# A hand-written step planner gets another transfer model, other durations, another order of bank choices and new weights, in an eight-layer hybrid transformer kernel

## The chip, the cores and the metric

One core of one Trainium2 chip runs the whole program. The metric is the device time of one execution in microseconds (us); lower is better. The names of the engines are those of the profile: PE is TensorE (PEld its weight loads), DVE is VectorE, ACT is ScalarE, POOL is GpSimd, SP is SyncE, whose only work here is to issue DMAs.

## The reference, cut to what matters

The input x has 4 batches of 1024 tokens with 128 features. Eight layers follow one another, each a residual around a layer norm, an attention or a feed-forward:

```
x = x + attn_a(layernorm(x))          # "full": 16 heads of 8, every query sees every key
x = x + ffn(layernorm(x))             # "ffn1": 128 -> 512 -> 128, relu
x = x + attn_b(layernorm(x))          # "causal" then "local" (window 32), 16 query and 4 key heads, rope, q and k normed
x = x + ffn(layernorm(x))             # "ffn2"
x = x + attn_padded(layernorm(x))     # "padded": window 32, 16 query and 2 key heads
x = x + moe(layernorm(x))             # "moe1": 8 experts, the best 2 for each token, width 352
x = x + attn_sink(layernorm(x))       # "sink": window 128 and 4 sink keys, 8 query and 4 key heads of 16
x = x + moe(layernorm(x))             # "moe2"
```

The batches do not depend on one another; the layers of one batch do.

## The kernel before, in words

`streams` describes the work of each batch as steps. A step (`Step`) has a list of pieces `on`, each an engine with a duration in nanoseconds, signals that it needs, and buffers that it takes from rings (`Ring`). `Plan.run` is a list scheduler that runs in Python while the program is built. It walks through its own time, and whenever an engine is free it picks, among the pieces that are ready and whose buffers can be had, the one that `urgency` puts highest. The order in which it picks becomes the order of the instructions in the queue of each engine, and the buffers that it picks are the ones that are used. On the chip the engines then run these queues in order and wait for semaphores. The plan's times are not used on the chip, only its orders, its choices of buffers and one more thing: where the plan sees PE idle, `tensor_program` puts matmuls on zeros (`nothing`, L1005 and L1007), one for each planned 230 ns after the first 200 or 450, at most 8 in a gap after the first 90 us.

`urgency` compares in this order: `short` (the engine of the step's next piece is about to run dry, by `SHORT`), then `step.far + step.lead + WORTH * stays`. `far` is the longest chain of planned durations and landings from the step to the end, in ns, so at most a few million. `lead` is 1000 times the sum of a number for the layer and batch (`LEADS`) and one for the kind of step (`URGENT`), so tens of millions. `WORTH` is a bonus for a PE step in the array mode that PE is in.

Transfers are planned in `Plan.go`. A step with DMAs gives for each the number of DMAs, a latency `ns` and an occupation `moved`. `moving` is the time at which the transfers planned so far are through:

```
for name, n, ns, moved in step.dmas(step):
    step.signals["dma"].name = name
    self.moving = max(self.moving, at) + moved
    self.due(step.signals["dma"], 16 * n, self.moving + ns)
```

Here `now` is when the issuing piece starts and `at` when it ends.

PSUM has 8 banks. `RB` gives pairs of neighbouring banks (for `scores` and `top`), and of the free pairs it takes the one free for longest. `RP` gives single banks from 7 downwards, for the accumulator `po` into which all products of a half unit of attention go. `RA` gives single banks from 7 downwards for short uses. All three share the same banks. `Step.room` goes through the rings of a step in the order in which they are named, so a ring that is named first chooses first.

An attention layer of a batch has 4 units. A unit is loaded (`load`, queries and keys from DRAM, where `split_out` put them as three bf16 parts), then in full, padded and sink the row maxima are found (`top` on PE at L1154 with its mask at L1134 or L1141, and `top` on DVE at L1609), then `scores` (PE L1185, mask L1134 or L1141) is followed by the exponential (ACT L1367), and `product` (PE L1205) adds up in `po`.

An experts layer (moe1, moe2) sorts the tokens of a batch into 23 tiles of 128 slots: 16 `scatter` DMAs by POOL (L1840), each pair after the one before has landed; `slot_load` brings 4 tiles from DRAM into a PT buffer (L1928), `slot_turn` transposes them (PE L1242, ACT L1384 into one of 3 SG buffers), `weights` brings each tile its expert (L1943, 384 KB), `up` (PE L1254, ACT L1389, DVE L1734 and L1737) and `down` (PE L1271, ACT L1402 into the same SG buffer) compute, `back` by POOL (L1848) scatters the rows to DRAM. An SG buffer is free when its `back` DMAs have landed. At the end `rows_in` (L1949) and `combine` (DVE L1745) add the rows to x. `zero` clears the slots in DRAM once for each batch (L1921).

Of the kernel before, what the change touches and what calls it, by code (L numbers as in the profile page):

```python
# [19 lines left out]
LEADS = dict(full=(33216, 19541, 25084, -10647), ffn1=(48012, -1595, 43514, 121701), causal=(-4228, -29528, -5475, 14633), local=(-22242, 1197, 39634, -30739), ffn2=(27232, 109504, 17203, 84270), padded=(6306, -51060, -19639, -27531), moe1=(7879, -27871, -29235, -11132), sink=(60610, 10946, -47942, -4076), moe2=(-46608, -58920, -16653, -27602))  # L20
URGENT = dict(back=13314, biased=-16184, combine=-8366, consts=50459, dest=-41354, divide_causal=-43734, divide_full=-14494, divide_local=-17929, divide_padded=-6368, divide_sink=-16411, down=32076, experts_in=-57783, gate_exp=-42278, gate_w=20450, k_padded=-30673, kv_global=-18223, latent=42087, load_causal=53214, load_full=-79031, load_local=-25554, load_padded=17122, load_sink=55523, mbd=6258, mixed=1379, narrow=2211, norm=-22134, ones=-2965, out=-4598, padding=41178, product_causal=158, product_full=33757, product_local=-27607, product_padded=-18694, product_sink=41317, project_causal=-26349, project_full=-64094, project_local=-22717, project_padded=188, project_sink=-10415, q_global=-64125, qk_rstd=-56931, qk_scaled=15461, qk_squares=-14285, qkv=-9555, ranks=-35465, residual=38685, route=-17061, rows_in=-41517, rstd=6282, scaled=-7356, scaled_dirs=-45906, scatter=-48392, scores_causal=13672, scores_full=807, scores_local=-10944, scores_padded=-11578, scores_sink=-265, sink_v=-6569, slot_load=53327, slot_turn=-10741, split_all=53562, split_hi=26458, split_lo=12833, split_out_causal=50567, split_out_full=-30502, split_out_local=-43483, split_out_padded=27921, split_out_sink=7305, squares=-60664, stats=-11217, store=-43970, top_full=8113, top_padded=-73, top_sink=7265, tops_full=-51182, tops_out_full=-35060, tops_out_padded=31757, tops_out_sink=-98863, tops_padded=352, tops_sink=-7328, tops_turn=82199, turn=11184, turn_add=6718, turn_mul=1696, up=-16818, v_full=10032, v_padded=54237, weights=17671, widen=24704, with_h=45447, zero=-17655)
SHORT = dict(pe=23620427, act=1123, dve=1280, pool=7696641590, sp=2084661)
ISSUE = 500
SWITCH = 100
WORTH = 2171223
# [89 lines left out]
class Plan:  # L115
# [3 lines left out]
    def __init__(self):  # L119
        self.count, self.order, self.steps = {}, {e: [] for e in ENGINES}, []  # L120
        self.free, self.ready, self.times = {e: 0 for e in ENGINES}, {e: [] for e in ENGINES}, set()
        self.banks = {}
        self.look, self.lead, self.coming, self.mode, self.moving = {}, 0, {e: 0 for e in ENGINES}, "whole", 0
# [16 lines left out]
    def add(self, *args, **given):  # L140
        step = Step(*args, **given)
        attention = step.given.get("A")
        step.lead = self.lead + 1000 * URGENT.get(step.kind + "_" + attention.name if attention else step.kind, 0)
# [14 lines left out]
    def urgency(self, step, i, now):  # L158
# [5 lines left out]
        return short, step.far + step.lead + WORTH * stays, -step.index  # L164

    def go(self, step, i, now):
# [1945 lines left out]
```

## Time and profile before

| | |
|---|---|
| median of 3 runs | 2376.72 us (2367.81 to 2389.58) |
| the profiled execution: its time, its span | 2365.46 us, 2363.7 us |
| PE busy | 2149.6 us (91%) |
| DVE busy | 1641.8 us (69%) |
| ACT busy | 1422.7 us (60%) |
| POOL busy | 674.2 us (29%) |
| share of the DMA engines' time, SP's queue | 31.5% |

The profile comes from one execution, whose span is from its first to its last instruction. An engine counts as busy while an instruction runs on it; the matmuls on zeros count as busy PE too. The idle time of an engine is put down to the instruction that came after it and to what released that instruction.

### The profile page before, as it was taken

What the parts mean: (1) busy time and instruction counts of PE and PEld (TensorE: products, weight loads), DVE (VectorE), ACT (ScalarE), POOL (GpSimd) and SP (SyncE); (2) the same over time, 40 slices, a digit from 0 to 9 for tenths busy, and PEclk for the clock granted to TensorE, in tenths of its full rate; (3) what the DMA queues carried; (4) which work ended last, traced back from release to release, by engine and by line L of the source; (5) the groups of instructions that cost most, each with busy time, mean ns of one, the idle gap of its engine ahead of it and who ended that gap; (6) DMA issues with size and microseconds to landing.
All of it is one profiled execution on the core that took longest, in us unless ns stands there. A gap on an engine that the chain in (4) does not pass through costs nothing.

```text
span 2363.7 us, 62948 instructions
## 1 busy us (share of the span) xinstructions
PE 2149.6 (91%) x26220; PEld 1224.9 (52%) x26243; DVE 1641.8 (69%) x3685; ACT 1422.7 (60%) x2105; POOL 674.2 (29%) x602
## 2 busy tenths in 40 slices
PE   7788988898999999899999999999999999999987
PEld 3222232223224233334554566697766887777987
DVE  9998879998876683423453388468687776866755
ACT  1367766666786889998777745644455234444333
POOL 4400000012002001203224214355515555424553
PEclk9999999999999999999999999999999999999998
DMA  6701100101121112112313324465624675634776
GB/s 189 222 18 35 41 17 17 44 17 50 27 50 45 25 34 65 51 23 68 92 47 87 78 48 113 106 204 158 184 50 117 188 222 168 192 101 123 229 240 195
DMA packets 160746, 235.23 MB, mean 100 GB/s; under 512 B 21968, under 2 KB 81872, under 8 KB 160208
## 3 DMA queue, kind: packets, MB, share of 16 engines
q1 hardware_dynamic: 145456, 206.81, 31.5%
q0 software_dynamic: 9984, 20.73, 2.5%
q8 instruction: 209, 3.42, 0.6%
q10 hardware_dynamic: 5024, 3.67, 0.6%
q14 instruction: 73, 0.60, 0.1%
HBM read 156.28 MB, written 73.88 MB: 97 GB/s over the span
## 4 chain that ended last, share of the span: by engine, by line
PE 56%; DVE 14%; ACT 11%; issue 7%; POOL 6%; DMA 5%; SPq 1%; POOLq 0%; DVEq 0%; ACTq 0%
PE PS L1205 16%; ACT PT L1367 10%; PE PS L1185 8%; DVE MS L1609 7%; PE PS L1154 5%; PE PS L1254 5%; DMA scr_y<-XN,SL 3%; PE PS L1141 3%; PE PS L1271 3%; PE PS L1054 2%; PE PS L1044 2%; POOL scr_o L1848 2%; PE PS L1015 2%; POOL scr_y L1840 2%; PE PS L1215 2%
## 5 line engine op out<-in xcount | busy, mean ns | idle before, releaser
L1367 ACT ACTIVATE PT<-PS 128x1024 f32<-128x1024 f32 (+5 forms) x1200 | 1018.6, 911 | 392.8 <-PE PS L1185 378.8
L1609 DVE TENSOR_REDUCE MS<-PS 128x2 f32<-128x1024 f32 (+3 forms) x736 | 778.2, 1097 | 141.4 <-PE PS L1154 136.1
L1205 PE MATMUL PS<-PT,VA 128*9 128x512 f32 (+7 forms) x6720 | 558.8, 434 | 14.3 <-ACT PT L1367 12.0
L1185 PE MATMUL PS<-QO,KO 64*64 64x512 bf16 (+7 forms) x6240 | 420.0, 305 | 47.0 <-ACT PT L1367 29.6
L1185 PEld LDWEIGHTS PS<-QO,KO 64*64 64x64 bf16 (+2 forms) x6240 | 177.5, 105 | 271.6 <-ACT PT L1367 130.9
L1154 PE MATMUL PS<-KO,QO 61*64 61x512 bf16 (+2 forms) x3520 | 286.4, 326 | 34.0 <-DVE MS L1609 16.6
L1254 PE MATMUL PS<-SG,WB 128*128 128x128 f32 x2208 | 276.1, 278 | 6.2 <-DMA WB<-in_mW 2.9
L1254 PEld LDWEIGHTS PS<-SG,WB 128*128 128x128 f32 x2208 | 261.8, 194 | 12.1 <-issue 7.3
L1154 PEld LDWEIGHTS PS<-KO,QO 61*64 61x64 bf16 (+1 forms) x3520 | 126.1, 104 | 243.4 <-DVE MS L1609 127.3
L1848 POOL DMA_INDIRECT scr_o<-SG,TO x184 | 182.0, 989 | 226.6 <-ACT SG L1402 197.4
L1205 PEld LDWEIGHTS PS<-PT,VA 128*9 128x9 f32 (+2 forms) x6720 | 127.8, 90 | 177.0 <-issue 115.4
L1788 POOL MEMSET VA<- 128x32 f32 (+2 forms) x20 | 3.7, 187 | 715.2 <-PE PS L1205 715.2
L1141 PE MATMUL PS<-c_half 64*64 64x128 bf16 (+4 forms) x2560 | 165.4, 279 | 24.0 <-ACT PT L1367 13.2
L1271 PE MATMUL PS<-W,HM 128*128 x1104 | 158.7, 283 | 16.8 <-DVE HM L1737 13.1
L1734 DVE SCALAR_TENSOR_TENSOR HM<-HM,PS 128x384 f32<-128x384 f32 x184 | 100.9, 548 | 94.8 <-ACT HM L1389 94.6
L1641 DVE RECIPROCAL RC<-PS 128x16 f32<-128x16 f32 x144 | 36.2, 252 | 178.9 <-PE PS L1215 178.8
L1840 POOL DMA_INDIRECT scr_y<-XN,SL x128 | 124.2, 971 | 122.3 <-DMA scr_y<-XN,SL 60.5
L1389 ACT ACTIVATE HM<-PS 128x384 f32<-128x384 f32 x184 | 90.4, 491 | 112.8 <-PE PS L1254 112.3
L1271 PEld LDWEIGHTS PS<-W,HM 128*128 128x128 f32 x1104 | 139.0, 194 | 26.3 <-issue 25.3
L1402 ACT ACTIVATE SG<-PS 128x128 f32<-128x128 f32 x184 | 51.1, 277 | 167.9 <-PE PS L1271 167.2
L1141 PEld LDWEIGHTS PS<-c_half 64*64 64x64 bf16 x2560 | 64.9, 104 | 145.9 <-ACT PT L1367 74.9
L1373 ACT ACTIVATE OB<-PS 128x512 f32<-128x512 f32 x144 | 88.0, 611 | 65.9 <-PE PS L1205 65.5
(182 smaller groups left out, 2474.7 us busy)
## 6 DMA issues: line engine op xcount, KB each, us to landing
WB<-in_mW SPq DMA_DIRECT2D x184, 384.0 KB
PT<-scr_y SPq DMA_DIRECT2D x40, 264.0 KB, 4.6
PT<-scr_o SPq DMA_DIRECT2D x16, 512.0 KB, 5.3
QO<-scr_q_full SPq DMA_DIRECT2D x32, 192.0 KB
KO<-scr_k_full SPq DMA_DIRECT2D x32, 192.0 KB
QO<-scr_q_causal SPq DMA_DIRECT2D x32, 192.0 KB
QO<-scr_q_local SPq DMA_DIRECT2D x32, 192.0 KB
QO<-scr_q_padded SPq DMA_DIRECT2D x32, 192.0 KB
```

The source lines that it names most:

```text
L1141: mm(pb[64 * c:64 * c + 64, h2, at:at + copies * width], C["identw"][r, :], rows, start=i == 0, stop=False, skip_group_check=True)
L1154: p = mm(pb[c:c + n, h2, at:at + kn], q[:, 128 * tt + c:128 * tt + c + n], k[:, k0:k0 + kn], start=not masked, stop=True, skip_group_check ...
L1185: p = mm(pb[c:c + n, h2, at:at + tn], k[:, k0 + c:k0 + c + n], q[:, t0:t0 + tn], start=not masked, stop=True, skip_group_check=masked)
L1205: p = mm(bank[32 * h:32 * h + D + 1, c0:c0 + tn], va[0:n, :], pt[0:n, plane, at:at + tn], start=s["first"] and j == 0, stop=s["last"] and ...
L1254: p = mm(pb[:, k, 128 * c:128 * c + 128], wt[:, at:at + 128], y, start=True, stop=True)
L1271: p = mm(RA[s.use["bank"].i][:, 0:128], hm[:, 128 * c:128 * c + 128], W3[:, bass.ds(first + 128 * c, 128)], start=c == 0, stop=c == 2)
L1367: e = activation(pt[0:r, 0:n, a:b], ps[0:r, 0:n, a:b], ACT.Exp, scale=s["A"].scale)
L1389: activation(HM[s.use["hm"].i][:, :], pair(s)[:, 0, 0:DW], ACT.Tanh, scale=0.5).then_inc(S["up_tanh"], 1)
L1609: v.tensor_reduce(to, got, AX.X, ALU.max).then_inc(S["top"], 1)
L1734: last(v.scalar_tensor_tensor(hm, hm, 1.0, pb[:, 0, 0:DW], ALU.add, ALU.mult))
L1840: p.indirect_dma_start(scr_y[b], bass.IndirectOffsetOnAxis(ap=SL[b][:, c, i:i + 1], axis=0), XN[:, i, 0:ROW], None).then_inc(S[s.signals[" ...
L1848: p.indirect_dma_start(scr_o[b], bass.IndirectOffsetOnAxis(ap=TO[b][:, t:t + 1], axis=0), SG[s["yt"].i][:, at:at + 128], None).then_inc(S[ ...
```

## The change

Transfers: the occupation now starts when the issuing piece starts (`now`), and the latency is added to the later of the end of the issue and the end of the occupation. The numbers of nearly all transfers change. Durations: `up` on PE from 1340 to 1385 ns, `down` from 670 to 755, and `product` 30 ns more for each block of keys after the first. Banks: the first `scores` of a chain names its accumulator ahead of its pair. Weights: all of `LEADS`, `URGENT`, `SHORT` and `WORTH` are new. `CHANGED` is empty and adds nothing; `lead` is computed from `plan.layer` and comes to the same formula. No instruction is added to or taken from a step; orders, buffers and matmuls on zeros follow from the plan.

```diff
-LEADS = dict(full=(33216, 19541, 25084, -10647), ffn1=(48012, -1595, 43514, 121701), causal=(-4228, -29528, -5475, 14633), local=(-22242, 1197, 39634, -30739), ffn2=(27232, 109504, 17203, 84270), padded=(6306, -51060, -19639, -27531), moe1=(7879, -27871, -29235, -11132), sink=(60610, 10946, -47942, -4076), moe2=(-46608, -58920, -16653, -27602))
+LEADS = dict(full=(53341, 36548, 37095, 4161), ffn1=(2644, -19651, 48946, 155384), causal=(5626, -23700, -8138, 18246), local=(-32503, 3959, -15293, -35192), ffn2=(34227, 133518, 50757, 136545), padded=(20383, -47193, 15851, 10637), moe1=(-10457, -25159, -18591, -12001), sink=(104327, 44402, -48211, 33771), moe2=(-57924, -103913, 2283, -11110))
+STRETCH, CHANGED = 100000, {}
...
-SHORT = dict(pe=23620427, act=1123, dve=1280, pool=7696641590, sp=2084661)
+SHORT = dict(pe=267476623, act=1084, dve=1269, pool=9525014120, sp=120267)
...
-WORTH = 2171223
+WORTH = 6579224
...
-                self.moving = max(self.moving, at) + moved
-                self.due(step.signals["dma"], 16 * n, self.moving + ns)
+                self.moving = max(self.moving, now) + moved
+                self.due(step.signals["dma"], 16 * n, max(self.moving, at) + ns)
...
-                    dmas=lambda s: [("%s_out%s" % (what, b), 3, 1500, 12 * r * n // 450)])
+                    dmas=lambda s: [("%s_out%s" % (what, b), 3, 1700, 3500 * r * n // 131072)])
...
-                        s = add("scores", cost, dict(load=U["load"]), dict(bank=RB, pt=PT, **chain) if po is None else dict(bank=RB, pt=PT),
+                        s = add("scores", cost, dict(load=U["load"]), dict(**chain, bank=RB, pt=PT) if po is None else dict(bank=RB, pt=PT),
...
-                    p = add("product", [("pe", int(1.667 * w) + 17, "product")], dict(v=v_ready, exp=[x["exp"] for x in was]), order=last,
+                    p = add("product", [("pe", int(1.667 * w) + 17 + 30 * (len(g["blocks"]) - 1), "product")], dict(v=v_ready, exp=[x["exp"] for x in was]), order=last,
...
-                        dmas=lambda s, n=n: [("q_in%s" % s.use["qo"].i, n, 1600, 4000 if not A.tiled else 2900 if A.group == 1 else 1800)])
+                        dmas=lambda s, n=n: [("q_in%s" % s.use["qo"].i, n, 1800, 7800 if not A.tiled else 6000 if A.group == 1 else 4500)])
```

The other new numbers, latency and occupation in ns, before and after; the issue is the duration of the issuing piece:

| step | issue | latency, occupation before | after |
|---|---|---|---|
| `zero` | 6000, then 500 | 15000, 0 | 1800, 5600 |
| `consts` | 1000 | 3000, 11000 | 1800, 7000 |
| `experts_in` | 500 | 3000, 9000 | 1900, 4600 |
| `scatter` | 2210 | 1500, 100 | 1500, 300 |
| `slot_load` | 500 | 2900, 900 | 1900, 1200 |
| `weights` | 450 | 1900, 1400 | 2100, 1300 |
| `back` | 960 | 2000, 50 | 1500, 300 |
| `rows_in` | 500 | 3000, 1850 | 2100, 2200 |
| `store` | 500 | 3000, 2000 | 2100, 1500 |

In `URGENT` 80 numbers change; of those that the text speaks of, `top_full` goes from 8113 to 18606, `split_hi` from 26458 to 55531, `scores_causal` from 13672 to 20993.

## Rows read from the trace of the kernel before

**Rows 1.** The page, busy time of each engine over the span

```profile
PE 2149.6 (91%) x26220; PEld 1224.9 (52%) x26243; DVE 1641.8 (69%) x3685; ACT 1422.7 (60%) x2105; POOL 674.2 (29%) x602
```

**Rows 2.** Busy time by stretch: stretch, length, then the engines

```profile
0.00:40.00 40.00, 25.93 (x139) 15.67 (x139) 35.38 (x124) 8.23 (x13) 15.88 (x21) 1.00 0.59 148
40.00:100.00 60.00, 46.51 (x326) 13.99 (x326) 59.12 (x64) 11.89 (x14) 34.74 (x16) 0.97 0.90 277
100.00:500.00 400.00, 348.06 (x3409) 100.54 (x3409) 352.23 (x427) 268.63 (x284) 9.34 (x10) 1.00 0.14 32
...
1700.00:2200.00 500.00, 474.32 (x5736) 383.31 (x5748) 374.89 (x1170) 217.24 (x402) 212.72 (x211) 0.99 0.50 148
...
2300.00:2364.00 64.00, 48.45 (x429) 47.53 (x427) 34.73 (x86) 19.97 (x50) 23.08 (x25) 0.89 0.65 199
```

**Rows 3.** The same stretches, matmuls on zeros alone (PE, PEld, POOL)

```profile
0.00:40.00 40.00, 10.55 (x43) 4.38 (x43) 0.21 (x1) 1.00 0.59 148
40.00:100.00 60.00, 21.04 (x67) 5.89 (x67) 0.00 (x0) 0.97 0.90 277
100.00:500.00 400.00, 23.80 (x74) 5.14 (x73) 0.00 (x0) 1.00 0.14 32
...
sum 2364.00, PE 81.31 PEld 23.90 POOL 0.21; mean PE 8.13 PEld 2.39 POOL 0.02
```

**Rows 4.** Waits of PE over the span: us in total, times, longest

```profile
PE PS L1185 <- ACT PT L1367: 29.6, 74, 1.5
...
PE PS L1154 <- DVE MS L1609: 16.6, 52, 0.7
PE PS L1154 <- ACT PT L1367: 13.6, 21, 0.9
PE PS L1141 <- ACT PT L1367: 13.2, 39, 0.6
PE PS L1271 <- DVE HM L1737: 13.1, 10, 3.9
PE PS L1185 <- DVE MS L1609: 12.2, 31, 0.6
...
PE PS L1134 <- ACT SG L1384: 4.9, 2, 3.8
...
PE PS L1242 <- DMA PT<-scr_y: 3.4, 1, 3.4
...
PE PS L1254 <- DMA WB<-in_mW: 2.9, 3, 1.4
PE PS L1254 <- ACT SG L1384: 2.6, 2, 2.4
```

**Rows 5.** Waits of ACT over the span

```profile
ACT SG L1384 <- DMA scr_o<-SG,TO: 30.7, 14, 5.0
```

**Rows 6.** The page, DMA issues: count, size, median us from issue to landing

```profile
PT<-scr_y SPq DMA_DIRECT2D x40, 264.0 KB, 4.6
PT<-scr_o SPq DMA_DIRECT2D x16, 512.0 KB, 5.3
...
scr_y<-HM SPq DMA_DIRECT2D x4, 1518.0 KB, 8.1
```

**Rows 7.** Line L1928, the 48 slot loads

```profile
DMA to landing us min/median/max: 2.6/4.6/7.2
```

**Rows 8.** Chain that ended last, 2291 to 2301 us: start, us, what

```profile
2291.07 4.74 DMA WB<-in_mW
...
2298.56 1.34 PE PS L1254 x12
2299.90 0.67 PE PS L1271 x6
```

**Rows 9.** Timeline of PE, 2282 to 2289 us: start, us, instruction, idle before

```profile
2282.43 1.64 PE L1271 MATMUL PS<-W,HM 128*128 x6 [3.89 <-DVE HM L1737]
...
2283.86 2.38 PE L1254 MATMUL PS<-SG,WB 128*128 128x128 f32 x12
...
2286.75 1.50 PE L1254 MATMUL PS<-SG,WB 128*128 128x128 f32 x12
```

More of the change, by code:

```diff
@@ L22 @@
-SHORT = dict(pe=23620427, act=1123, dve=1280, pool=7696641590, sp=2084661)
+LEADS = dict(full=(53341, 36548, 37095, 4161), ffn1=(2644, -19651, 48946, 155384), causal=(5626, -23700, -8138, 18246), local=(-32503, 3959, -15293, -35192), ffn2=(34227, 133518, 50757, 136545), padded=(20383, -47193, 15851, 10637), moe1=(-10457, -25159, -18591, -12001), sink=(104327, 44402, -48211, 33771), moe2=(-57924, -103913, 2283, -11110))
+STRETCH, CHANGED = 100000, {}
+URGENT = dict(back=6321, biased=12423, combine=-30114, consts=71223, dest=-35934, divide_causal=-46876, divide_full=-14842, divide_local=-10228, divide_padded=5133, divide_sink=-25331, down=54974, experts_in=-45597, gate_exp=-19345, gate_w=43937, k_padded=-27108, kv_global=-36694, latent=37451, load_causal=55136, load_full=-98931, load_local=-64659, load_padded=44073, load_sink=48910, mbd=-27211, mixed=-22633, narrow=-21902, norm=-11253, ones=-381, out=-2013, padding=50769, product_causal=784, product_full=28059, product_local=-33836, product_padded=-9477, product_sink=32951, project_causal=-43056, project_full=-57538, project_local=-19091, project_padded=11700, project_sink=-12956, q_global=-85021, qk_rstd=-44870, qk_scaled=14611, qk_squares=-18579, qkv=-47915, ranks=-56805, residual=23888, route=-33480, rows_in=-59941, rstd=23560, scaled=1588, scaled_dirs=-66840, scatter=-25435, scores_causal=20993, scores_full=3298, scores_local=-8686, scores_padded=-15878, scores_sink=-8616, sink_v=7800, slot_load=67324, slot_turn=-4593, split_all=44198, split_hi=55531, split_lo=7723, split_out_causal=78242, split_out_full=-8892, split_out_local=-44055, split_out_padded=47993, split_out_sink=15080, squares=-68676, stats=-14713, store=-17676, top_full=18606, top_padded=7164, top_sink=1941, tops_full=-42818, tops_out_full=-29746, tops_out_padded=25651, tops_out_sink=-100701, tops_padded=-14612, tops_sink=-13606, tops_turn=86466, turn=19652, turn_add=18956, turn_mul=-11213, up=-26800, v_full=3177, v_padded=54005, weights=34310, widen=31222, with_h=32524, zero=11167)
@@ L122, in __init__ @@
         self.banks = {}
-        self.look, self.lead, self.coming, self.mode, self.moving = {}, 0, {e: 0 for e in ENGINES}, "whole", 0
+        self.look, self.layer, self.coming, self.mode, self.moving = {}, None, {e: 0 for e in ENGINES}, "whole", 0
     def given(self, name, value, at):
@@ L142, in add @@
         attention = step.given.get("A")
-        step.lead = self.lead + 1000 * URGENT.get(step.kind + "_" + attention.name if attention else step.kind, 0)
+        step.name, step.layer = step.kind + "_" + attention.name if attention else step.kind, self.layer
+        step.lead = 1000 * (LEADS[step.layer[0]][step.layer[1]] if step.layer else 0) + 1000 * URGENT.get(step.name, 0)
         self.steps.append(step)
@@ L163, in urgency @@
         stays = engine == "pe" and step.mode[0] == self.mode
-        return short, step.far + step.lead + WORTH * stays, -step.index
+        changed = CHANGED.get(now // STRETCH, {})
+        return short, step.far + step.lead + 1000 * (changed.get(step.name, 0) + changed.get(step.layer, 0)) + WORTH * stays, -step.index
     def go(self, step, i, now):
@@ L804, in experts @@
                 if t % GROUP == 0:
-                    load = add("slot_load", [("sp", ISSUE, "")], dict(y=placed), dict(pt=PT), leaves=dict(PT=2), b=b, t=t, n=n, dmas=lambda s, t=t: [("y_in%s_%s" % (b, t // GROUP), 1, 2900, 900)])
+                    load = add("slot_load", [("sp", ISSUE, "")], dict(y=placed), dict(pt=PT), leaves=dict(PT=2), b=b, t=t, n=n, dmas=lambda s, t=t: [("y_in%s_%s" % (b, t // GROUP), 1, 1900, 1200)])
                     s = add("slot_turn", [("pe", 110 * n, "slot_turn_mm"), ("act", 568 if n == GROUP else 465, "slot_turn")], dict(y=[load["dma"]]),
@@ L820, in experts @@
                 group["order"].append(s)
-                down = add("down", [("pe", 670, "down_mm"), ("act", 160, "rows")],
+                down = add("down", [("pe", 755, "down_mm"), ("act", 160, "rows")],
                            dict(src=[s["gated"]], w=experts_in, slots=slots),
@@ L826, in experts @@
                 s.use["hm"].give(down["down_mm"])
-                back = add("back", [("pool", 960, "")], dict(rows=[down["rows"]], to=[to["dest"]]), b=b, t=t, yt=group["yt"], dmas=lambda s: [("back%s" % s["yt"].i, 1, 2000, 50)])
+                back = add("back", [("pool", 960, "")], dict(rows=[down["rows"]], to=[to["dest"]]), b=b, t=t, yt=group["yt"], dmas=lambda s: [("back%s" % s["yt"].i, 1, 1500, 300)])
                 group["back"].append(back["dma"])
@@ L834, in experts @@
             for c in range(2):
[L835 removed]
+                got = add("rows_in", [("sp", ISSUE, "")], dict(rows=returned), dict(pt=PT), b=b, c=c, dmas=lambda s, c=c: [("g_in%s_%s" % (b, c), 1, 2100, 2200)])
                 s = add("combine", [("dve", 2200, "combine")], dict(got=[got["dma"]], w=wt, x=prev), b=b, c=c, pt=got.use["pt"])
@@ L841, in batch @@
         to_x = into_x()
-        plan.lead = 1000 * LEADS["full"][b]
+        plan.layer = ("full", b)
         attention(ATT["full"], lambda A: full_prologue(A, to_x), to_x)
         state["x"] = to_x["ready"]
-        plan.lead = 1000 * LEADS["ffn1"][b]
+        plan.layer = ("ffn1", b)
         feed_forward()
-        plan.lead = 1000 * LEADS["causal"][b]
+        plan.layer = ("causal", b)
         attention(ATT["causal"], causal_prologue, None)
-        plan.lead = 1000 * LEADS["local"][b]
+        plan.layer = ("local", b)
         attention(ATT["local"], local_prologue, None)
```

28 lines of the change are left out of this document (13 added, 15 removed).

## The prediction, made before any run of the changed kernel

> **What bounds the kernel now.** I read the busy shares first. PE is busy for 2149.6 us of 2363.7 [rows 1], so 214.1 us are idle. Of the busy time 81.3 us are matmuls on zeros, which the plan puts where it sees PE idle [rows 3]. PE's own work is thus 2149.6 - 81.3 = 2068.3 us, and 295.4 us of the span is PE time without work. The change leaves the work alone, so all that it can win or lose is in these 295.4 us. The reader should next see where they lie, from the table by stretch [rows 2] with the zeros beside it [rows 3]:
>
> - 0 to 100 us: idle 14.1 + 13.5, zeros 10.6 + 21.0, together 59.2. DVE is busy for 59.1 of the 60 us after 40, so the start is a chain of norms, splits and maxima on DVE.
> - 100 to 500 us: idle 51.9, zeros 23.8, together 75.7. DVE is busy for 352 of 400 us: the maxima of full attention.
> - 1700 to 2200 us: idle 25.7 in 500 us, 5%. The experts and the sink attention of different batches hide one another.
> - 2300 us to the end: 15.6 idle, nearly all of it after the last `down`, when only `back`, `rows_in`, `combine` and `store` are left.
>
> The rest, 295.4 - 59.2 - 75.7 - 25.7 - 15.6 = 119 us, is spread over the other stretches and the remaining zeros. Then I read what ended PE's waits [rows 4]. The costliest are waits for a bank pair or for an exponential: scores and maxima behind ACT L1367 or DVE L1609, 29.6 + 16.6 + 13.6 + 13.2 + 12.2 = 85.2 us. Waits that a landing ended itself are 3.4 + 2.9 = 6.3 us. Landings also act through ACT: `slot_turn` waits 30.7 us for the `back` DMAs that free its SG buffer [rows 5], the next tile's tanh stands behind it in ACT's queue, and PE's `down` behind that: 13.1 + 4.9 + 2.6 = 20.6 us [rows 4]. So what a wrong landing costs PE today is at most 6.3 + 20.6 = 27 us.
>
> **The change part by part.** The sum is made against the profiled execution, 2365.5 us, which is 11.3 us under the median of 2376.7; I add that back at the end.
>
> **Landings.** Both models can be worked out for a transfer that finds the queue empty, from the start of the issue. A load of full attention (6 issues of 500): before 3000 + 2900 + 1600 = 7500 ns, after max(6000, 3000) + 1800 = 7800. A `slot_load`: 500 + 900 + 2900 = 4300, after 1200 + 1900 = 3100. A `rows_in`: 5350, after 4300. A `weights`: 3750, after 3400. `zero`: 6000 + 15000 = 21000, after 7400. Against the trace: the `zero` landed in 8.1 us, so the new number is right where the old was far off; the slot loads landed in 4.6 us and `rows_in` in 5.3 at the median [rows 6], so there the old numbers are nearer and the new ones short by 1.5 and 1.0 us, unless the shared queue adds the rest. It can: the old occupation of a full load was 2.9 us, the new one is 6.0, so more transfers will find the queue taken. The fastest slot load took 2.6 us [rows 7], which says that an empty queue is quicker than either number.
>
> The Trainium skill (page "DMA: Bandwidth & Descriptors", section "Anatomy of one DMA — SWDGE (gpsimd) path") gives a fixed part of about 2.0 us and bytes over 436 GB/s, which by that rule makes an estimated 2.6 us for 264 KB. The trace agrees for the fastest slot load, 2.6 us [rows 7], and not for the median of 4.6 [rows 6]. If the rule were the whole truth, the new landings would be late enough everywhere and the rival below that loses by them would cost nothing.
>
> What the landings win: half of the 27 us above, 13, because orders that know when an SG buffer comes free put other work there, and because a wait can't vanish where POOL's own queue is the cause. Bounds: nothing, and 27. What they cost: a `slot_turn` that is put 1.5 us too early stops PE for up to 1.5 us. The old number was short by 0.3 and one such wait of 3.4 us is all that PE shows [rows 4], in a stretch where other batches fill 95% of PE's time [rows 2]. I take 5 us, between 0 and 48 x 1.5 = 72 us, near the low end, as the row of 3.4 us is the nearest.
>
> **Expert durations.** In the chain a tile's `up` takes 1.34 us and its `down` 0.67 when they follow one another [rows 8], which are the old 1340 and 670. The new plan counts 45 + 85 = 130 ns more for each of 184 tiles, 24 us of plan time. On the chip they take what they take: 0 us of their own. It makes the plan believe that PE is the late engine, so it puts fewer zeros there, and what it believes of the other engines stays on the safe side. I count nothing, between -3 (some zeros of the experts' stretches go) and +3.
>
> **Accumulator ahead of pair.** Once in each chain of products (4 attention layers x 4 batches x 4 units x 2 halves = 128, and sink 4 x 2 x 2 = 16, together 144) the accumulator now takes the highest free bank, and the pair what is left; before, the pair could take bank 7 and push the accumulator into the middle, where it stays for the whole half unit and splits the free banks so that fewer pairs fit. The trace doesn't name banks. The bound is what PE waits for banks and exponentials, 85.2 us [rows 4]. But the pairs are not aligned before or after (the pair free for longest may be 1 and 2), and that splits the banks too, and part of the 85.2 is DVE and ACT being slow rather than a missing pair: in 100 to 500 us DVE is 88% busy [rows 2]. I take a tenth, 9 us; bounds 0 and 85. Below nothing I see no more than the 9 us again, if a pair that is left over is one that was freed last.
>
> **New weights.** They dominate the order: `far` is a few million, differences of `LEADS` and `URGENT` are tens of millions, so old and new are nearly fixed lists of priorities. `WORTH` of 6.6 million instead of 2.2 stays small beside them. `SHORT` of PE and POOL exceeds the whole plan before and after, and the values for ACT and DVE move by 3% and 1%. Two groups of moves can be read. First, full attention rises by 15 to 20 million, `top_full` by 10 and `split_hi` by 29, so all of the start is pressed harder; but there DVE is busy for 59.1 of 60 us, and an order can't shorten it: 0 us. Second, the layers of a batch spread differently, which decides whether DVE's maxima meet PE's feed-forwards and experts. The pool is 51.9 idle + 23.8 zeros from 100 to 500 us and the 119 us of the rest, together 195. All steps move, their DMAs in SP's queue and the `scatter` and `back` steps in POOL's with them. With a model of the same kind but nearer durations I expect about 7% of that, 14 us; bounds: a tenth more idle time (+20) and a fifth less (-39). This is the least certain term and no row fixes it.
>
> Sum: -13 + 5 + 0 - 9 + 0 - 14 = -31 us. 2365.5 - 31 = 2334.5 by the profiled execution, and 2334.5 + 11.3 = 2345.8 at the level of the median. I say **2346 us**, 1.3% less. What would be late next: from 100 to 500 us DVE, at the end the chain from the last scatters through 23 tiles of 2.01 us to the store, which this change touches only if another batch comes last.
>
> **The clock.** Once near the end PE stood idle for 3.89 us, and the 12 matmuls of the next `up` took 2.38 us instead of 1.50 [rows 9]: after that idle time they ran in part at the lower of the clock's two levels, 1.2 GHz. Over long stretches it costs little: granted is 0.89 of the upper level, 2.4 GHz, from 2300 us on and 0.97 to 1.00 elsewhere in [rows 2]. A new order with more gaps of that size would pay 0.9 us more for each. With some ten waits behind ACT and DVE in the experts' stretches [rows 4] this is at most 10 us either way, and is inside the bounds of the last term.
>
> **The rivals.** First, no change to speak of: the landings won and lost cancel (-13 + 13), the accumulators are worth nothing since misaligned pairs split the banks anyway, and the new order wins 5 us, since it moves idle time from one stretch to another. For it: DVE near its limit in the early stretches, and PE already at 95% where the experts are. Time 2372, between 2353 and 2400.
>
> Second, slower: the landings are too short where the queue is busy. The place is the experts' stretches, where a tile asks for 384 KB every 2 us; one load of weights there took 4.74 us [rows 8] against a planned 3.4, and slot loads take 4.6 against 3.1 [rows 6]. PE runs its queue in order, so an `up` or `slot_turn` put too early stops everything behind it, attention of other batches too. If each of the 48 slot loads costs 1.0 us and one in ten of the 184 weights 1.3, that is 48 + 24 = 72 us; the other terms win 13 + 9 + 14 = 36, which leaves +36: 2376.7 + 36 = 2413 us. It decides from the point where PE waits for DMA by more than 60 us in all, against 6 today. Against it: the shared queue makes up for part of what the latencies lost, and SG and PT buffers let loads run ahead.
>
> Third, a larger gain: the missing pairs were what held PE, so half of the 85.2 us goes, and the weights reach their bound of 39: 43 + 39 and the landings' 13 - 5 = 8, 90 us less: 2287 us. For it: 85.2 us is the largest group of PE's waits. Against it: DVE is 88% busy from 100 to 500 us.
>
> Fourth, the change doesn't do what it says: the new numbers are read by the planner alone, and if its picks didn't depend on them the time would be 2376.7. The weights make that impossible for the order as a whole; for landings and accumulators alone it lies in the first rival.
>
> **How the numbers follow.** Forecast, 2320 to 2353: 0.42. First rival: 0.27. Second: 0.18. Third, under 2320: 0.13. A measurement of this kernel tells no change from about 1% (its three runs spread over 0.9%), so faster means under 2353, slower over 2400. Faster is 0.42 + 0.13 = 0.55, same 0.27, slower 0.18. The range leaves out 2 in 10: it ends at 2400, which leaves out the 0.18 of the slower case, and begins at 2290, which leaves out a few hundredths of the third case.
>
> **What the profile after would show.** Landings right: ACT's wait of 30.7 us for SG buffers falls under 20 and PE's waits for `up` and `down` with it; wrong: PE waits for PT or WB landings by tens of us. Accumulators: the 85.2 us of waits for pairs fall by about 9, with the same DVE busy time. Weights: idle time plus zeros from 100 to 500 us falls under 75. In all, work stays at 2068 us and time without work falls from 295 to about 264. I would be wrong above all by the last term: if it has the other sign, the sum is near nothing; and if the plan's improvement is larger than a search on the old model left room for, the third rival is what is seen.

## The result, and the profile after

The changed kernel takes 2406.7 us (median of 4 runs, 2401.5 to 2412.2) where the kernel before takes 2373.4 beside it: ratio 1.0135, 95% interval 1.0108 to 1.0163. Two later comparisons gave 1.0105 (1.006 to 1.015) and 1.0132 (1.0091 to 1.0174). So it is 1.0 to 1.35% slower, and the forecast of 2346 us, with its range up to 2400, was wrong in sign.

The profiled execution took 2412.2 us (span 2410.3); its span is 46.6 us longer than that of the profiled one of before (2365.5, span 2363.7). It is the slowest of its runs, and before's was 7.9 us under its median, so sizes read from the pair are somewhat large. Line numbers after are those of before plus 3. The page's busy times, then the table by stretch (stretch, length, engines, granted clock as a share of 2.4 GHz, DMA), then the same table for matmuls on zeros:

```profile
PE 2180.9 (90%) x26203; PEld 1239.6 (51%) x26203; DVE 1642.4 (68%) x3685; ACT 1421.7 (59%) x2105; POOL 675.6 (28%) x602
```

```profile
40.00:100.00 60.00, 48.82 (x301) 13.60 (x300) 58.74 (x63) 7.98 (x10) 30.86 (x14) 0.86 0.87 255
100.00:500.00 400.00, 354.50 (x3463) 100.61 (x3459) 357.78 (x431) 273.77 (x289) 15.59 (x14) 1.00 0.15 36
...
1500.00:1700.00 200.00, 180.53 (x2089) 151.71 (x2080) 128.23 (x382) 81.74 (x172) 108.61 (x103) 0.94 0.56 166
1700.00:2200.00 500.00, 459.23 (x5632) 367.64 (x5633) 348.75 (x1053) 206.70 (x382) 200.53 (x197) 0.97 0.46 136
2200.00:2300.00 100.00, 89.58 (x781) 84.00 (x780) 69.11 (x277) 37.36 (x85) 51.68 (x55) 0.93 0.71 214
2300.00:2411.00 111.00, 87.14 (x747) 84.59 (x745) 54.82 (x134) 35.42 (x88) 49.46 (x52) 0.93 0.68 203
```

```profile
100.00:500.00 400.00, 21.28 (x70) 4.68 (x70) 0.00 (x0) 1.00 0.15 36
...
sum 2411.00, PE 73.02 PEld 20.20 POOL 0.20; mean PE 7.30 PEld 2.02 POOL 0.02
```

Two stretches of before that [rows 2] leaves out:

```profile
1500.00:1700.00 200.00, 186.56 (x2413) 158.83 (x2402) 134.90 (x397) 91.97 (x189) 109.73 (x104) 0.99 0.60 178
...
2200.00:2300.00 100.00, 88.36 (x743) 85.28 (x742) 59.47 (x194) 35.18 (x87) 58.82 (x63) 0.97 0.75 230
```

The reader should see where the two part. From 100 to 500 us PE is busier after than before [rows 2]. From 1500 us on, in the experts' stretches, PE is busy for 180.5 of 200 us instead of 186.6 and for 459.2 of 500 instead of 474.3, at a lower granted clock. PE's work without zeros is 2180.9 - 73.0 = 2107.9 us against 2068.3, though the instructions are the same: 39.6 us more at a mean clock of 0.974 against 0.990. Idle time is 229.4 against 214.1, and zeros are 8.3 less: 39.6 + 15.3 - 8.3 = 46.6. So the time without work, idle and zeros together, grew only from 295.4 to 302.4 us. Two more profiles of the changed kernel (`again_after` and `after_third` below) show the same: PE's own work is 25.2 and 33.9 us above before's, at a clock of 0.980 and 0.975, and the time without work is 294.2 and 298.9.

PE's waits, and the waits behind the experts' DMAs:

```profile
PE PS L1018 <- DVE XN L1467: 32.4, 9, 12.9
PE PS L1188 <- ACT PT L1370: 27.4, 65, 0.9
PE PS L1144 <- ACT PT L1370: 18.0, 44, 1.7
PE PS L1274 <- DVE HM L1740: 16.6, 15, 4.3
PE PS L1157 <- DVE MS L1612: 16.2, 48, 0.9
...
PE PS L1188 <- DVE MS L1612: 10.8, 26, 1.3
PE PS L1157 <- ACT PT L1370: 9.1, 17, 0.9
...
PE PS L1245 <- DMA PT<-scr_y: 4.7, 2, 4.2
PE PS L1245 <- ACT SG L1387: 4.6, 1, 4.6
```

```profile
POOL scr_y L1843 <- DMA scr_y<-XN,SL: 64.3, 39, 5.5
ACT SG L1387 <- DMA scr_o<-SG,TO: 41.3, 16, 6.3
DVE XN L1467 <- DMA scr_y<-XN,SL: 31.1, 6, 11.9
```

The last line of before, and PE's wait behind it after 1400 us, before and then after:

```profile
DVE XN L1464 <- DMA scr_y<-XN,SL: 18.6, 6, 5.2
```

```profile
PE PS L1015 <- DVE XN L1464: 5.3, 3, 2.4
```

```profile
PE PS L1018 <- DVE XN L1467: 17.3, 6, 5.1
```

The waits for pairs and exponentials, 85.2 us before [rows 4], are now 27.4 + 18.0 + 16.2 + 10.8 + 9.1 = 81.5. ACT's wait for `back` DMAs rose from 30.7 [rows 5] to 41.3. PE's own waits for landings stay at some 10 us in all. What grew most is PE's wait for the normed tokens in XN: DVE can't write them before the scatters that read the XN buffer have landed. All of PE's waits after 1400 us, summed over that view, are 54.7 us in 74 before and 84.3 in 83 after; 80.3 in 76 in another execution of the changed kernel. They are little more in number, but longer. Two of them in PE's timeline (start, length, instruction, idle before it):

```profile
1965.05 1.09 PE L1245 MATMUL PS<-c_first,PT 128*128 128x128 f32 x4 [4.63 <-ACT SG L1387]
```

```profile
2250.19 1.64 PE L1274 MATMUL PS<-W,HM 128*128 x6 [4.34 <-DVE HM L1740]
2251.62 2.77 PE L1257 MATMUL PS<-SG,WB 128*128 128x128 f32 x12
```

After 4.34 us without work the next `up` took 2.77 us, as after the 3.89 us of before [rows 9]: part of it ran at 1.2 GHz. That is one way in which idle time turns into more busy time.

### The profile page after: what moved, and what is told of

It is laid out like the page before. It is cut to its first block, busy times and chain, and to the rows that moved or that the text cites. A ratio compares the mean times of both kernels' runs of the same rounds, so it can differ in the third digit from the quotient of the medians.

```text
span 2410.3 us, 62915 instructions
## 1 busy us (share of the span) xinstructions
PE 2180.9 (90%) x26203; PEld 1239.6 (51%) x26203; DVE 1642.4 (68%) x3685; ACT 1421.7 (59%) x2105; POOL 675.6 (28%) x602
## 3 DMA queue, kind: packets, MB, share of 16 engines
q1 hardware_dynamic: 145456, 206.81, 30.7%
## 4 chain that ended last, share of the span: by engine, by line
PE 55%; DVE 13%; ACT 11%; DMA 7%; issue 7%; POOL 7%; SPq 0%; POOLq 0%; DVEq 0%; ACTq 0%
PE PS L1208 15%; ACT PT L1370 9%; PE PS L1188 8%; DVE MS L1612 7%; PE PS L1157 5%; PE PS L1257 5%; DMA scr_y<-XN,SL 4%; PE PS L1144 3%; POOL scr_y L1843 3%; PE PS L1047 2%; PE PS L1057 2%; PE PS L1274 2%; PE PS L1018 2%; PE PS L1218 2%; POOL scr_o L1851 2%
## 5 line engine op out<-in xcount | busy, mean ns | idle before, releaser
L1208 PE MATMUL PS<-PT,VA 128*9 128x512 f32 (+8 forms) x6720 | 563.0, 437 | 12.3 <-ACT PT L1370 11.0
L1188 PE MATMUL PS<-QO,KO 64*64 64x512 bf16 (+6 forms) x6240 | 424.0, 307 | 42.0 <-ACT PT L1370 27.4
L1188 PEld LDWEIGHTS PS<-QO,KO 64*64 64x64 bf16 (+1 forms) x6240 | 180.0, 106 | 276.1 <-ACT PT L1370 130.6
L1157 PE MATMUL PS<-KO,QO 61*64 61x512 bf16 (+2 forms) x3520 | 289.6, 329 | 28.2 <-DVE MS L1612 16.2
L1257 PE MATMUL PS<-SG,WB 128*128 128x128 f32 x2208 | 285.8, 283 | 10.2 <-ACT SG L1387 5.9
L1257 PEld LDWEIGHTS PS<-SG,WB 128*128 128x128 f32 x2208 | 269.8, 198 | 17.6 <-issue 12.9
L1843 POOL DMA_INDIRECT scr_y<-XN,SL x128 | 124.9, 976 | 126.1 <-DMA scr_y<-XN,SL 64.3
```

What stands on the lines that cost most here:

```text
L1157: p = mm(pb[c:c + n, h2, at:at + kn], q[:, 128 * tt + c:128 * tt + c + n], k[:, k0:k0 + kn], start=not masked, stop=True, skip_group_check ...
L1188: p = mm(pb[c:c + n, h2, at:at + tn], k[:, k0 + c:k0 + c + n], q[:, t0:t0 + tn], start=not masked, stop=True, skip_group_check=masked)
L1208: p = mm(bank[32 * h:32 * h + D + 1, c0:c0 + tn], va[0:n, :], pt[0:n, plane, at:at + tn], start=s["first"] and j == 0, stop=s["last"] and ...
L1257: p = mm(pb[:, k, 128 * c:128 * c + 128], wt[:, at:at + 128], y, start=True, stop=True)
L1843: p.indirect_dma_start(scr_y[b], bass.IndirectOffsetOnAxis(ap=SL[b][:, c, i:i + 1], axis=0), XN[:, i, 0:ROW], None).then_inc(S[s.signals[" ...
```

## The experiments

Chips differ: before took about 2373 us on some and 2420 on others, so each kernel is compared with before on the same chip. One figure beside the runs is not from a chip: the **planned end**, the time at which the planner's own clock says that the last step ends. It is 2288.9 us for before and 2303.1 for the changed kernel. The **distance** is the median on the chip less the planned end; I compare it with before's distance on the same chip. The intervals of the ratios make each such difference uncertain by about 8 to 11 us.

**Each part alone, with the weights that stood beside it.** Theories: the parts act alone as I had costed them; or weights fit one set of numbers, and any change of one without the other scatters the plan.

```
p1_landings   only the dmas=... numbers and the shared queue in go()
p2_durations  only up 1385, down 755, product + 30 * (blocks - 1)
p3_banks      - dict(bank=RB, pt=PT, **chain)   + dict(**chain, bank=RB, pt=PT)
p4_weights    only LEADS, URGENT, SHORT, WORTH
```

> The kernel before with the new transfer model and its numbers alone; durations, bank choice and weights stay old. Theory 1 (short landings are to blame): the loss of 33 us comes with the landings, so about 2400 to 2420 us. Theory 2 (orders are chosen by weights that fit one set of numbers, and any change of a number without weights found for it scatters the plan): the plan itself, by its own times, ends at 2467.9 us instead of 2288.9, and the chip at 2500 us or more.

> The kernel before with the new PE durations of up, down and product alone. Theory 1 (landings): no loss, 2365 to 2390 us. Theory 2 (weights fit one set of numbers): the plan ends by its own times at 2451.9 us, and the chip at 2500 us or more.

> The kernel before with the accumulator choosing its bank ahead of the pair, alone. Theory 1 (landings): no loss, perhaps the 9 us of gain of the prediction, 2355 to 2380 us. Theory 2 (weights fit one set of numbers): the plan ends by its own times at 2451.5 us, and the chip at 2500 us or more.

> The kernel before with the new LEADS, URGENT, SHORT and WORTH alone; the planner's numbers and bank choice stay old. Theory 1 (landings): no loss, 2350 to 2390 us. Theory 2 (weights fit one set of numbers): the plan ends by its own times at 2451.8 us, and the chip at 2500 us or more.

Measured, one execution each, before 2423.8 beside them: 2597.8, 2534.8, 2600.5 and 2582.2 us, 4.6 to 7.3% slower. The planner had foreseen it: its planned ends are 2467.9, 2451.9, 2451.5 and 2451.8. The second theory holds. A part of this change has no effect of its own; parts can be compared only with weights searched for each. The bank choice alone, which I had put at -9 us with a bound of +9, came out 177 us slower through the order that it upset.

**The changed kernel once more, and zeros.** A third theory: the lower clock after is the cause, and zeros at the places where PE idles unplanned would win the time back.

```
+ MORE = {66: 4, 1210: 13, ...}   # place in PE's order: further zeros
- for _ in range(min(n, 8 if s.idle_at > 90000.0 else 150)):
+ for _ in range(min(n, 8 if s.idle_at > 90000.0 else 150) + MORE.get(place, 0)):
```

`z_after` has 257 zeros more in the changed kernel, `z_before` 130 more in before, `z_none` is before with none after 90 us.

> The changed kernel once more, on the chip on which the three kernels with other matmuls on zeros run, so that they can be compared with it. All theories: 1.35% over the kernel before, 2400 to 2415 us if that kernel is at 2370.

> The changed kernel, same orders and buffers, with 257 more matmuls on zeros put at the 24 places where its trace shows PE idle for more than 1.2 us (together 66 us). Theory 3 (the loss is the clock: the new durations leave fewer zeros in the experts' stretches, PE falls to 1.2 GHz after unplanned gaps, and its work takes some 26 us longer there): PE no longer falls, granted clock 0.99 or more, time 20 to 26 us less than the changed kernel, 2380 to 2390 us. Theory 1 (landings are planned too short, the gaps themselves are the loss): the gaps stay, so at most 5 to 10 us less.

> The kernel before, with 130 more matmuls on zeros at the 17 places where its trace shows PE idle for more than 1.2 us (together 36 us). Theory 3 (clock): its granted clock is 0.990 already, so 5 to 10 us less, 2360 to 2368 us. Theory 1: no change that can be told.

> The kernel before without any matmul on zeros after the first 90 us (136 fewer in the plan), same orders and buffers. Theory 3 (clock): granted clock falls to 0.97 and the time rises by 20 us or more, 2390 to 2400 us. Theory 1: the zeros matter little, within 10 us of the kernel before.

Measured, before 2373.3: `again_after` 2398.5, `z_after` 2412.3 (1.015, 1.0114 to 1.0186), `z_before` 2373.3 (0.9995, 0.9977 to 1.0014), `z_none` 2378.5 (1.0011, 0.9989 to 1.0033). In the traces the zeros are 139.1 us of PE's time in `z_after` against 72.8 in `again_after`, and the clock 0.985 against 0.980. PE's own work fell from 2093.5 to 2072.7 us, nearly before's 2068.3, but the time without work rose from 294.2 to 336.3, and nothing was won. In `z_none` the zeros are 31.1 against 81.3 with a clock of 0.980 against 0.990; PE's own work is 29.6 us longer, and next to nothing was lost. So more zeros don't win the loss back, and a lower clock alone, as in `z_none`, hardly costs time. What the clock is worth by itself isn't shown, since `z_after` pays for it with zeros.

**No wait between scatters.** The scatters of a batch wait for one another's landings (64.3 us on POOL above). If landings planned too short delay the changed kernel there, taking the wait away should help it more than before.

```
-                w.wait_all(s.needs["landed"])
```

> The kernel before, same plan, orders and buffers, without the wait of each scatter pair for the landing of the pair before (all sixteen of a layer still land before any slot is loaded). Theory 1 in its sharper form (the landings that the plan has too short are above all those of the scatter chain: planned 3.71 us for a pair, 1.26 + 3.7 = 4.96 us in the trace, eight pairs in a row, eight times): the lag of the chip behind the plan shrinks by up to 8 x 8 x 1.25 = 80 us where nothing hides it; I expect 15 to 40 us less, 2335 to 2358 us. Theory 4 (lateness is spread over everything, and the scatter chain is hidden by the other batches): within 8 us of the kernel before.

> The changed kernel, same plan, orders and buffers, without that wait. Sharper theory 1: the changed order is the one that the late scatters hurt more, so it gains more than the kernel before does, 30 to 60 us, and comes within 15 us of the kernel before without the wait. Theory 4: it gains no more than the kernel before does, and stays 1% to 1.3% behind it.

Measured, before 2425.3: `s_before` 2457.6 (1.0132, 1.0102 to 1.0162), `s_after` 2460.4 (1.0133, 1.0096 to 1.0171). Both theories missed it: without the wait, before is 1.3% slower. Its trace shows where part of it goes. Busy time by stretch, `s_before` in its first run of scatters, then before in its own:

```profile
1488.39:1506.07 17.68, 6.28 (x104) 2.74 (x96) 1.89 (x2) 0.77 (x2) 13.67 (x14) 0.63 0.15 50
```

```profile
1484.95:1522.90 37.95, 35.57 (x969) 23.69 (x965) 14.08 (x44) 26.72 (x49) 19.52 (x21) 1.00 0.41 102
```

POOL, SP and PE of `s_before` there, and the DMA queues of `s_before` from 1488 to 1508 us and of before from 1485 to 1523:

```profile
1493.71 0.95 POOL L1839 DMA_INDIRECT scr_y<-XN,SL  x1 [0.31 <-issue]
1494.97 0.96 POOL L1839 DMA_INDIRECT scr_y<-XN,SL  x1 [0.30 <-issue]
1496.24 0.96 POOL L1839 DMA_INDIRECT scr_y<-XN,SL  x1 [0.30 <-issue]
```

```profile
1480.28 32.77 SPq L1915 DMA_DIRECT2D QO<-MTd  x4
```

```profile
1494.17 0.37 PE L1154 MATMUL PS<-KO,QO 61*64 61x160 bf16 x4 [1.00 <-issue]
...
1495.60 0.33 PE L1141 MATMUL PS<-c_half 64*64 64x128 bf16 x3 [1.03 <-issue]
...
1502.49 0.32 PE L1141 MATMUL PS<-c_half 64*64 64x128 bf16 x4 [5.14 <-issue]
```

```profile
DMA packets 448, 0.95 MB, mean 47 GB/s; under 512 B 224, under 2 KB 224, under 8 KB 448
...
q0 software_dynamic: 448, 0.95, 14.3%
```

```profile
q1 hardware_dynamic: 1814, 2.72, 31.0%
q0 software_dynamic: 480, 1.01, 8.9%
q8 instruction: 7, 0.11, 1.4%
q14 instruction: 1, 0.01, 0.1%
```

While POOL issues 14 scatters without a pause, one each 1.26 us, no packet of any other queue moves, those that bring instructions among them, and PE is busy for 6.3 of 17.7 us, mostly waiting for nothing but its own issue. SP wasn't out of work: its four DMA issues of L1915 stretch over 32.8 us, against 15.7 in before. With the wait the scatters spread over 38 us, the other queues move 1822 packets, and PE is busy for 35.6. That trace is from a faster chip; `n_old` below, with the wait and on a slow one, has 14 scatters in 29.6 us, 908 packets of other queues from 1500 to 1531 us, and PE busy for 23.1. The stall is the only run of 14; most later scatters of `s_before` still come in pairs, the longest other run is of 8, and the rest of the 32 us wasn't traced. The comparison also says that the two orders, 1.0 to 1.35% apart with the wait, are level without it (2457.6 and 2460.4 us).

**New orders, old landings and new.** Now the weights were searched anew for each planner. Theory A: landings planned too short cost time on the chip. Theory B: any order found anew lags more than before's, whatever its landings. Edits, beside LEADS and URGENT (SHORT and WORTH are the changed kernel's):

```
n_old    none
s_short  slot_load 2900 -> 1900, rows_in 3000 -> 2000, back 2000 -> 1000, weights 1900 -> 900, scatter 1500 -> 500
l_long   the same five + 1000: 3900, 4000, 3000, 2900, 2500
c_long   changed planner with old durations; slot_load 1900 -> 2900, rows_in 2100 -> 3100,
         back 1500 -> 2500, weights 2100 -> 2600, scatter 1500 -> 2000
```

> Planner as before (its landings, durations, bank choice), but with other weights: searched from the changed kernel's weights until the planned end was 2300.2 us (before's is 2288.9, the changed kernel's 2303.1 by its own numbers). Distance from the planned end to the time on the chip: before 84 us, the changed kernel 96 to 110. Theory A (landings planned too short cost on the chip): a new order under the old landings keeps before's distance, so 2384 us where before takes 2373, ratio 1.005. Theory B (before's order is simply a lucky one, and any newly found order lags more, whatever its landings): distance 100 to 110, ratio 1.012 to 1.015.

> Planner as before, with five landings of the experts' stretches 1000 ns shorter (slot_load, rows_in, back, weights, scatter), weights searched anew until the planned end was 2300.6 us. Theory A: distance 105 us or more, 2405 or more where before takes 2373, ratio 1.014 or more, and clearly above n_old, whose planned end is the same. Theory B: equal to n_old.

> As s_short with the same five landings 1000 ns longer than before's instead; planned end 2315.3 us. Theory A: distance 65 to 75 us, 2380 to 2390 where before takes 2373, ratio 1.003 to 1.007. Theory B: distance 100 to 110, 2415 to 2425, ratio 1.018 to 1.022.

> The changed kernel's planner with the old durations and with four landings of the experts lengthened towards the trace (slot_load 2900, rows_in 3100, back 2500, scatter 2000, weights 2600 ns after the queue), weights searched from the changed kernel's for a low planned end under three sets of landings; planned end 2307.4 us. Theory A: distance 70 to 85, 2377 to 2392 where before takes 2373, ratio 1.002 to 1.008, faster than the changed kernel. Theory B: 2407 to 2417, ratio 1.014 to 1.018.

And on another chip, with the changed kernel beside them:

```
m_land   only the change's landings      b_bank   only the change's bank choice
a_other  the whole changed planner, other weights
```

> The changed kernel itself, beside the three below on one chip; planned end 2303.1 us. Distances from planned end to chip are compared with before's in this call. Both theories: its distance is 13 to 19 us more than before's, ratio 1.011 to 1.014.

> Only the landings of the change, with weights searched for them from the changed kernel's (planned end 2317.9 us; durations and bank choice of before). n_old, a new order under the old landings, lay 14.6 us further from its plan than before's. Theory A (the new landings, in the experts' stretches too short, cost time on the chip on top of what any new order lags): distance at least 25 us more than before's, ratio 1.023 or more. Theory B (a newly found order lags some 15 us more than before's, and the new landings add nothing to it): distance 8 to 20 us more, ratio 1.015 to 1.020.

> Only the accumulator ahead of the pair, with weights searched for it from the changed kernel's (planned end 2319.7 us; landings and durations of before). Both theories: distance as n_old's, 8 to 20 us more than before's, ratio 1.016 to 1.021. More than that would say that the bank choice makes orders that the chip follows worse.

> The whole change of the planner with other weights (searched from n_old's, planned end 2331.5 us). Theory A: distance at least 25 us more than before's, ratio 1.028 or more. Theory B: 8 to 20 us more, ratio 1.021 to 1.026.

```
             planned   chip     ratio to before (95%)     distance less before's
n_old        2300.2   2444.4   1.0098 (1.0064-1.0132)     144.2 - 129.6 = +15
s_short      2300.6   2481.3   1.0257 (1.0213-1.0301)     180.7 - 129.6 = +51
l_long       2315.3   2443.5   1.0110 (1.0074-1.0146)     128.2 - 129.6 =  -1
c_long       2307.4   2452.0   1.0130 (1.0090-1.0169)     144.6 - 129.6 = +15
after_third  2303.1   2404.7   1.0132 (1.0091-1.0174)     101.6 -  83.2 = +18
m_land       2317.9   2423.3   1.0201 (1.0160-1.0243)     105.4 -  83.2 = +22
b_bank       2319.7   2415.7   1.0176 (1.0132-1.0219)      96.0 -  83.2 = +13
a_other      2331.5   2421.5   1.0205 (1.0163-1.0248)      90.0 -  83.2 =  +7
```

`s_short` and `n_old` have the same planned end and lie 37 us apart on the chip, more than theory A's 20; `l_long` keeps before's distance. In the table by stretch, `n_old`, `s_short` and `l_long` from 1700 to 2200 us:

```profile
1700.00:2200.00 500.00, 456.13 (x5563) 368.54 (x5564) 347.67 (x1038) 199.85 (x385) 207.73 (x201) 0.97 0.48 140
```

```profile
1700.00:2200.00 500.00, 441.71 (x5374) 350.26 (x5373) 342.14 (x993) 197.58 (x374) 191.02 (x181) 0.95 0.47 138
```

```profile
1700.00:2200.00 500.00, 452.36 (x5507) 354.39 (x5504) 351.20 (x1028) 201.38 (x374) 205.88 (x196) 0.98 0.46 135
```

PE's waits after 1400 us sum to 100.4, 121.8 and 91.5 us. So an order searched on landings 1 us shorter lost time, in the stretch that theory A names. One searched on landings 1 us longer won none: `l_long` and `n_old` are level on the chip (2443.5 and 2444.4), and what makes its distance small is a planned end 15 us later. Of the expectations that I gave, B's held for `b_bank`, and `n_old`, `c_long`, `m_land` and `a_other` ended just outside its ranges (1.0098 for 1.012 or more, 1.013 for 1.014 or more, 1.0201 for 1.020 or less, 1.0205 for 1.021 or more); A's held for `s_short`; `l_long` fell between the two. No version here beats before.

**The orders under one set of numbers.** The distance has a flaw: each planned end is reckoned with its own planner's numbers, and short numbers make it early by themselves. The planner can also walk through an order that is already fixed, engine queues and buffers kept, under another set of numbers. This is reckoned from the runs' kernels and not measured; on its own numbers each order comes back to within 4 us of its planned end. Ends in us, with the difference to before's order, beside the difference of the medians on the chip:

```
             before's numbers   changed numbers   chip
before       2291.8             2327.1
after        2314.6   +23       2303.8   -23      +25 to +33
n_old        2303.5   +12       2338.5   +11      +26
s_short      2343.4   +52       2372.8   +46      +63
l_long       2309.9   +18       2344.5   +17      +25
c_long       2317.5   +26       2329.2    +2      +34
m_land       2338.6   +47       2342.5   +15      +51
b_bank       2319.8   +28       2348.1   +21      +44
a_other      2346.2   +54       2334.4    +7      +49
```

The reader should compare the signs for the changed kernel. By the changed numbers its order is 23 us better than before's; by the old numbers it is 23 us worse, and the chip agrees with the old. They also rank the eight new orders nearly as the chip's ratios do (`a_other` and `s_short` change places, and the changed kernel's 1.0105 to 1.0135 can't be told from `l_long` and `c_long`), and miss the chip's differences by 16 us at most. The changed numbers miss them by up to 57. Of the change, the transfer model and its numbers alone turn +23 into -10; the new durations alone turn it into +10. So theory A's mechanism is the one that the reckoning supports: the search found an order that is good by transfer numbers that the chip doesn't bear out. No run on the chip isolates this, and `n_old`, searched on the old numbers, is 1.0% slower than before too.

## Why the prediction was wrong

The result is about +32 us: beside `after_third`, 2404.7 - 2372.1 = 32.6. By the planned ends it splits into 14.2 us that the plan itself ends later (2303.1 against 2288.9, each by its own numbers) and 18.4 us more distance from plan to chip; in `again_after` the second part was 11.

- **New weights, the step that failed.** I took -14 us, since a search against "a model of the same kind but nearer durations" should end in a better order. The instructions are the same, so the loss is in the order, and the whole change measured +25 to +33, outside the bound of +20. New weights for the old numbers (`n_old`) cost 26 us by themselves. Two premises were wrong. The model wasn't nearer: by before's numbers, with which the chip agrees better, the order that the new weights make ends 23 us later, and only the changed numbers see it 23 us earlier. And I had treated the old weights as what any search leaves, with 7% of 195 us still to win; all eight newly searched orders are slower than before's, on the chip and by the old numbers.
- **Work stays at 2068 us**, and only the 295 us without work can change, I wrote. PE's own work measured 2093.5 to 2107.9 us in three profiles and the time without work 294.2 to 302.4.
- **Landings.** -13 and +5 were my terms. The gain isn't seen: ACT's wait for `back` rose to 41.3 instead of falling under 20. My bound of 27 us for what wrong landings cost PE also left out the path through DVE's XN buffers, where PE's wait after 1400 us rose from 5.3 to 17.3 us (15.8 and 20.2 in the two other profiles), and of its 20.6 us only the 13.1 is a wait of `down`. The slot loads land in 4.1 us at the median and `rows_in` in 5.9, against 4.6 and 5.3 before, so "short by 1.5 and 1.0 us" stands at 1.0 and 1.6 now. By the reckoning the cost of such numbers came through the search, which is the term above; PE's waits for slot loads, which I had priced, went only from 3.4 to 4.7 us. Landings after (count, KB, median us):

```profile
WB<-in_mW SPq DMA_DIRECT2D x184, 384.0 KB, 4.1
PT<-scr_y SPq DMA_DIRECT2D x40, 264.0 KB, 4.4
PT<-scr_o SPq DMA_DIRECT2D x16, 512.0 KB, 5.9
```

- **Accumulator ahead of the pair.** -9 was forecast; the waits for pairs and exponentials fell by 3.7 us (85.2 to 81.5), and `b_bank`, with weights of its own, ended 1.8% over before. No gain is shown.
- **Durations**, 0: not run with weights of their own. Reckoned without them, the changed order ends 8.5 us earlier (2295.3 for 2303.8) and before's gains 22 (2304.9 for 2327.1), so they too bent the search towards the new order, by 14 us.
- **100 to 500 us** would fall under 75 us without work, I wrote: it is 45.5 idle + 21.3 zeros = 66.8. This came true, but PE's waits after 1400 us rose from 54.7 to 84.3, which is more than it gave.
- **The rivals.** The slower one (0.18) had the sign, the place and nearly the time (2413), not the mechanism: its condition, over 60 us of PE waiting for DMA, was not met (`PT<-scr_y` is 4.7 us), so the stalls came through ACT and DVE; that the time came near was in part luck. The rule of the Trainium skill that I quoted (page "DMA: Bandwidth & Descriptors", section "Anatomy of one DMA — SWDGE (gpsimd) path") makes an estimated 2.6 us for 264 KB. It is stated for DMAs issued by GpSimd, and these are issued by SP. The fastest of the 48 slot loads took 2.6 us again, the median of its rows is 4.1 to 4.4.
- **The clock**, at most 10 us either way: as busy time too small, since PE's own work grew by 25 to 40 us while the clock fell from 0.990 to 0.974 to 0.980. As elapsed time it isn't refuted: `z_after`, `z_before` and `z_none` moved zeros by 66, 39 and 50 us and the time by at most 0.6% (2412.3 against 2398.5), and more zeros never made it shorter.

**What stays open.** By before's numbers seven of the eight new orders should lag before's less than they do, by 2 to 16 us. A part of that is noise, the rest has no cause here. That the lead is gone without the wait between scatters points to how before's order lays work beside POOL's DMAs, but this wasn't isolated. Nor was it tried to give the changed kernel a search as long as before's may have had.

## What to carry to other kernels

When a planner's numbers and weights change together, the numbers have no effect of their own: what they do is to decide which order the search takes for a good one. Before searching on new numbers, walk orders that have already been timed through the planner under the old and the new numbers, and keep the set that ranks them as the chip did. Two planned ends that come from different numbers, like the two here that lie 14 us apart, can't be set against each other. Landings planned 1 us short lost 37 us against an order of equal planned end, and landings 1 us longer neither lost nor won. And before a wait between indirect DMAs is taken away, look at what the other queues move in its pauses.

## What the runs showed of the hardware

- A run of 14 indirect DMAs from POOL at one each 1.26 us left every other queue, instructions included, without a packet for 20 us, with PE busy for 6.3 of 17.7 us (`s_before`). With a wait for the landing between pairs PE was busy for 35.57 of 37.95 us over 16 of them on a faster chip, and for 23.1 of 29.6 over 14 on a slow one (`n_old`).
- Removing 50 us of zeros from a kernel with PE 91% busy lowered the mean clock from 0.990 to 0.980 and moved the time by 0.1% (0.9989 to 1.0033), though PE's own work took 29.6 us longer in the trace.
- The same program took 1.9 to 2.2% longer on two chips (2418 to 2425 us) than on others (2372 to 2373). All ten traces from the two show waits that have no recorded releaser, and none of the ten from the others does. Two such lines, over the span of `n_old`:

```profile
ACT SG L1405 <- remote: 38.6, 16, 4.6
ACT HM L1392 <- remote: 21.0, 10, 5.2
```
